# Expert down product with the activations held: four products of 128 columns a chunk, sum with tokens in partitions

## The reference, cut to what matters

```
probs = softmax(x @ gate_w.T)                     # 32 experts
comb  = the 8 largest of probs, over their sum    # 0 elsewhere
for each expert e (width 64):
    g, u = split(x @ gate_up_w[e].T, 2)
    out += (u * silu(g)) @ down_w[e].T * comb[:, e]
```

## Time and profile before

| | |
|---|---|
| median of 3 runs | 1034.54 us (1033.78 to 1035.93) |
| the profiled execution | 1029.92 us, span of the instructions 1028.2 us |
| mean granted clock of TensorE in it | 0.982 |
| TensorE, weight loads | 918.5 us busy, 631.6 us (they overlap) |
| VectorE, ScalarE, POOL | 645.9, 613.9, 658.5 us busy |
| down product (L1438) | 512 MATMULs, 263.5 us busy |
| the turn of its sum (L1359) | 64 MATMULs, 9.7 us busy |
| its copy (L1000) | 16 times, 9.5 us busy |

### The profile page before, as it was taken

One profiled execution on the slowest core, in us unless ns is written; L12 is line 12 of the kernel. 1 busy time (PEld: TensorE's weight loads), 2 busy tenths in 40 slices (PEclk: granted clock), 3 DMA queues, 4 the chain that ended last, 5 costly groups with the idle time before them and its releaser, 6 DMA issues.

```text
span 1028.2 us, 16655 instructions
## 1 busy us (share of the span) xinstructions
PE 918.5 (89%) x5472; PEld 631.6 (61%) x5472; DVE 645.9 (63%) x1444; ACT 613.9 (60%) x1869; POOL 658.5 (64%) x607
## 2 busy tenths in 40 slices
PE   3237898998999999999999999999999998999998
PEld 1024565676666566677666565678666576667665
DVE  5884785668757856778748745778744247447432
ACT  3236475687394566698475556699355459377432
POOL 5763768556668856856759855857655546645654
PEclk9998999889999999999999999999999999999999
DMA  5004343102543525530353524550153652261352
GB/s 179 1 0 96 82 85 83 42 25 53 134 104 82 117 62 123 124 83 18 76 112 83 125 55 93 119 115 18 42 126 83 125 124 55 51 144 26 83 126 61
DMA packets 63224, 85.67 MB, mean 83 GB/s; under 512 B 3681, under 2 KB 29090, under 8 KB 62882
## 3 DMA queue, kind: packets, MB, share of 16 engines
q1 hardware_dynamic: 63138, 84.61, 36.6%
HBM read 79.32 MB, written 5.28 MB: 82 GB/s over the span
## 4 chain that ended last, share of the span: by engine, by line
PE 61%; ACT 15%; DVE 6%; POOL 6%; issue 5%; DVEq 0%; ACTq 0%; POOLq 0%
PE bank L1438 17%; PE bank L1412 9%; PE bank L1414 8%; PE bank L1413 8%; ACT probs L1008 6%; PE bank L1474 3%; PE bank L1459 3%; PE bank L1488 2%; POOL work L826 2%; PE bank L1310 1%; PE bank L1316 1%; PE bank L1452 1%; ACT work L984 1%; DVE probsT L1256 1%; POOL probs L834 1%
## 5 line engine op out<-in xcount | busy, mean ns | idle before, releaser
L826 POOL TENSOR_TENSOR work<-work,spread_w 128x512 f32<-128x512 f32 x256 | 336.5, 1327 | 184.5 <-DVE work L1215 168.7
L1215 DVE TENSOR_TENSOR work<-work,bank 128x512 f32<-128x512 f32 x256 | 174.3, 682 | 234.4 <-ACT work L984 151.7
L1438 PE MATMUL bank<-work,down_w 128*128 128x512 f32 x512 | 263.5, 598 | 9.0 <-ACT yT L1000 5.6
L984 ACT ACTIVATE work<-bank 128x512 f32<-128x512 f32 x256 | 151.0, 596 | 183.1 <-PE bank L1414 180.3
L1008 ACT ACTIVATE probs<-bank,neg_max 128x96 f32<-128x96 f32 x512 | 166.0, 385 | 10.6 <-DVE neg_max L1242 9.0
L1412 PE MATMUL bank<-z_hi,gate_hi 128*128 128x512 f32 x256 | 168.9, 660 | 0.0
L834 POOL TENSOR_TENSOR probs<-probs,prob_inv 128x768 f32<-128x768 f32 x64 | 94.1, 1471 | 74.7 <-DVE prob_inv L1250 74.7
L1008 ACT ACTIVATION_READ_ACCUMULATOR probs<-bank,neg_max 128x1 f32 x512 | 127.3, 251 | 0.0
L1438 PEld LDWEIGHTS bank<-work,down_w 128*128 128x128 f32 x512 | 95.3, 190 | 38.1 <-POOL work L826 9.8
L1414 PE MATMUL bank<-z_hi,gate_lo 128*128 128x512 f32 x256 | 102.7, 401 | 0.0
L1412 PE MATMUL bank<-z_hi,up_hi 128*128 128x512 f32 x256 | 102.1, 399 | 0.0
(11 more groups left out here) (142 smaller groups left out, 1484.3 us busy)
## 6 DMA issues: line engine op xcount, KB each, us to landing
spread_w<-comb_dram SPq DMA_DIRECT2D x128, 512.0 KB, 6.7
vals<-v_dram SPq DMA_DIRECT2D x16, 384.0 KB, 4.1
x_buf<-x SPq DMA_DIRECT2D x8, 256.0 KB, 3.4
v_dram<-v_tok SPq DMA_DIRECT2D x8, 256.0 KB, 4.7
out<-xs SPq DMA_DIRECT2D x8, 256.0 KB, 3.8
spread_w<-wg SPq DMA_DIRECT2D x1, 1024.0 KB, 7.2
spread_w<-wu SPq DMA_DIRECT2D x1, 1024.0 KB, 9.2
comb_dram<-combT SPq DMA_DIRECT2D x16, 64.0 KB, 1.6
```

What stands on the lines that cost most here:

```text
L826: pool.tensor_tensor(work[:, n % WORK], work[:, n % WORK], spread_w[:, n // EACH % 2, s % EACH], ALU.mult).then_inc(hid_gated, 1)
L984: act.activation(work[:, n % WORK], bank[GATE_BANKS[ring_of(row, f, s)]], ACT.Silu).then_inc(silu_ready, 1)
L1215: dve.tensor_tensor(work[:, n % WORK], work[:, n % WORK], bank[UP_BANKS[ring_of(row, f, s)]], ALU.mult).then_inc(gated_ready, 1)
L1438: pe.matmul(bank[Y_BANK], down_w[:, c], work[:, n % WORK], start=(c == 0), stop=(c == CH - 1)).then_inc(down_done, 1)
```

## The change

The down product holds 128 tokens of `work` and streams `down_w[:, c]`, four times a chunk. The sum has tokens in partitions, as x has. The copy and the turn go, with `yT`, `y_copied` and the y_back steps of all tables. VectorE adds bank 6 to x directly (y_add), and this add now frees bank 6: the first down product of a stage and the first mix of an attention part wait for `moe_done`. y_add stands where y_copy stood in time, but on VectorE: at slot 3 before gated, in an attention part behind the maxima of the second tile.

```diff
@@ scalar
-            def y_copy(fg):
-                act.wait_ge(down_done, (fg + 1) * CH)
-                act.activation(yT[:], bank[Y_BANK], ACT.Copy).then_inc(y_copied, 1)
...
-                        if s == LAG and not starts_stream(row, f):
-                            y_copy(STAGE_AT[row, f] - 1)
...
-                        if i == f[0]:
-                            y_copy(end - 1)
...
-            y_copy(len(STREAM) - 1)
@@ vector
-            def y_back(row, f):
-                x = x_of(row) if f < G else xs
-                add_side(x, x, f % G, row, "y_back", f, moe_done, STAGE_AT[row, f] + 1)
+            def y_add(fg):
+                row, f = STREAM[fg]
+                dve.wait_ge(down_done, (fg + 1) * CH)
+                x = (x_of(row) if f < G else xs)[:, T * (f % G):T * (f % G) + T].rearrange("p t d -> p (t d)")
+                dve.tensor_tensor(x, x, bank[Y_BANK], ALU.add).then_inc(moe_done, 1)
...
+                        if s == LAG and not starts_stream(row, f):
+                            y_add(STAGE_AT[row, f] - 1)
...
+                        if i == f[0]:
+                            y_add(END_AT[row, i] - 1)
...
-            y_back(ROWS - 1, MOE - 1)
+            y_add(len(STREAM) - 1)
@@ tensor
-            def y_back(row, f):
-                pe.wait_ge(y_copied, STAGE_AT[row, f] + 1)
-                side_free(row, "y_back", f)
-                for t in range(T):
-                    mm = pe.transpose(side[:, P * t:P * (t + 1)], yT[:, P * t:P * (t + 1)], ident[:])
-                mm.then_inc(side_ready, 1)
...
-                    wait(pe, y_copied, n // CH)
+                    wait(pe, moe_done, n // CH)
...
-                pe.matmul(bank[Y_BANK], down_w[:, c], work[:, n % WORK], start=(c == 0),
-                          stop=(c == CH - 1)).then_inc(down_done, 1)
+                for t in range(T):
+                    cols = slice(P * t, P * (t + 1))
+                    mm = pe.matmul(bank[Y_BANK][:, cols], work[:, n % WORK, cols], down_w[:, c], start=(c == 0 and t == 0),
+                                   stop=(c == CH - 1 and t == T - 1), skip_group_check=True)
+                mm.then_inc(down_done, 1)
...
-                    pe.wait_ge(y_copied, END_AT[row, i])
+                    pe.wait_ge(moe_done, END_AT[row, i])
```

More of the change, by code:

```diff
@@ L64 @@
 Y_BANK, SIDE_BANK = 6, 7
-IN_SIDE = ("x_turn", "qkv", "attnT", "mlp1", "mlp2", "moe_turn", "route", "weighT", "y_back",
+IN_SIDE = ("x_turn", "qkv", "attnT", "mlp1", "mlp2", "moe_turn", "route", "weighT",
            "seq_turn", "keys", "queries", "values", "proj")
@@ L112 @@
         8: own(("route", 1), ("r_sum", 1)) + ahead(("wred", 1)),
-        9: own(("top", 1), ("y_back", 0)),
+        9: own(("top", 1)),
         10: own(("weigh", 1)) + ahead(("kvsum", 2)),
@@ L126 @@
         4: back(("m_apply", 3)) + ahead(("h_newton2", 0), ("h_rg", 0)),
-        5: back(("y_back", 2)) + ahead(("h_scale", 0)),
+        5: ahead(("h_scale", 0)),
         6: back(("moe_turn", 3), ("z_hi", 3)) + ahead(("h_sq2", 0)),
@@ L144 @@
         4: ahead(("m_apply", 0)),
-        5: own(("y_back", 1)) + ahead(("kvsum", 5)),
+        5: ahead(("kvsum", 5)),
         6: ahead(("moe_turn", 0), ("z_hi", 0)) + own(("s_stats", 1), ("s_rstd", 1)),
@@ L157 @@
     "attn": {
-        8: back(("y_back", 3)),
         26: own(("proj", 0)),
@@ L161 @@
     "attn_lo": {
-        5: own(("y_back", 1)),
         6: own(("s_stats", 1), ("s_rstd", 1)),
@@ L165 @@
     "attn_hi": {
-        5: back(("y_back", 3)),
     },
@@ L194 @@
         3: ahead(("h_scale", 0), ("qscale", 1), ("attend", 4)),
-        4: own(("y_back", 0)) + ahead(("h_sq2", 0)),
+        4: ahead(("h_sq2", 0)),
         5: own(("s_stats", 0), ("s_rstd", 0)) + ahead(("h_red2", 0), ("h_pow2", 0)),
@@ L210 @@
         2: own(("s_rstd", 1)),
-        3: own(("y_back", 1), ("s_stats", 1)),
+        3: own(("s_stats", 1)),
         4: own(("s_apply", 1)) + ahead(("attend", 6)),
@@ L254 @@
         9: own(("route", 1), ("r_sum", 1)) + ahead(("wred", 1)),
-        10: own(("top", 1), ("y_back", 0)),
+        10: own(("top", 1)),
         11: own(("weigh", 1)) + ahead(("kvsum", 2)),
@@ L267 @@
         4: ahead(("h_newton1", 0)),
-        5: back(("y_back", 2), ("m_apply", 3)) + ahead(("x_turn", 1), ("h_newton2", 0), ("h_rg", 0)),
+        5: back(("m_apply", 3)) + ahead(("x_turn", 1), ("h_newton2", 0), ("h_rg", 0)),
         6: own(("values", 0)) + ahead(("h_scale", 0)),
@@ L288 @@
         4: back(("m_apply", 3)),
-        5: back(("y_back", 2)) + own(("queries", 0)),
+        5: own(("queries", 0)),
         6: back(("moe_turn", 3), ("z_hi", 3)),
@@ L325 @@
     (ROWS, "fourth"): {
-        5: back(("y_back", 2)),
     },
@@ L407, in every_step @@
             yield from slot_steps(period, place, at)
-    yield ROWS - 1, "y_back", MOE - 1
 ORDER = list(every_step())
@@ L483, in hybrid_block @@
         work = sb("work", [P, WORK, GT])
-        yT = sb("yT", [P, GT])
         seqT, keysT = sb("seqT", [P, WIN + SEQ]), sb("keysT", [P, WIN + SEQ])
@@ L528, in hybrid_block @@
         silu_ready, gated_ready, hid_gated = sem("silu_ready"), sem("gated_ready"), sem("hid_gated")
-        down_done, y_copied, moe_done = sem("down_done"), sem("y_copied"), sem("moe_done")
+        down_done, moe_done = sem("down_done"), sem("moe_done")
         scores_ready, max_ready, probs_ready = sem("scores_ready"), sem("max_ready"), sem("probs_ready")
@@ L1220, in _ @@
                      "h_red1": h_red1, "h_newton1": h_newton1, "h_newton2": h_newton2, "h_scale": h_scale, "h_red2": h_red2, "h_sum": h_sum, "mlp2": mlp2,
-                     "z_lo": z_lo_step, "r_sum": r_sum, "top": top_step, "comb": comb_step, "y_back": y_back, "proj": proj, "lead": lambda row, n: gated(row, 0, n)}
+                     "z_lo": z_lo_step, "r_sum": r_sum, "top": top_step, "comb": comb_step, "proj": proj, "lead": lambda row, n: gated(row, 0, n)}
             norm_stats(0, "x", 0)
@@ L1418, in _ @@
                      "seq_turn": lambda row, n: turn(row, "s", n, "seq_turn"), "qkv": qkv_step, "attnT": attnT_step,
-                     "mlp1": mlp1, "mlp2": mlp2, "route": route, "weighT": weighT, "y_back": y_back, "keys": keys,
+                     "mlp1": mlp1, "mlp2": mlp2, "route": route, "weighT": weighT, "keys": keys,
                      "queries": queries, "values": values, "proj": proj,
```

## The result

The changed kernel takes 1058.99 us in the median (1044.99 to 1080.40, four runs), the one before 1034.16 in the same series. The ratio is 1.0225, 95% interval 1.0158 to 1.0293: 2.2% slower, where 0.8% had been forecast, and outside the range. The profiled execution of the changed kernel is its slowest, 1080.40 us; a second profile, of 1058.11 us, stands among the experiments (after again) and is nearer to the median. The ratios in this document leave out runs more than 1.5% above the fastest of their kernel (here the one of 1080.40), so they differ a little from the quotients of the medians.

What follows compares the result with a forecast made beforehand. TensorE was taken to bound the expert stages, TensorE and ScalarE by turns the attention parts. 12 - 4.4 - 1.5 - 6.4 + 7 + 3 - 1.35 = +8.4, say +8 us: 1042.5 us, range 1032 to 1051.

Steps and rivals of the forecast that it cites:

- term 2: Transposes of the sum leave TensorE: -4.4 us in expert slots, -1.5 in attention parts; late reciprocal against freed ScalarE: 0.
- rival C: First attention part's half clock lasts longer or shows elsewhere: +6 us, 1048 us, chance 0.14; gone: 6 less, chance 0.04.
- Term 1: Down product in expert stages: four products for one cost 0.05 us a chunk over 256 chunks, loads hidden, +12 us.
- Rival D: Down product's weight loads do not hide: six more per chunk paid in full, +292 us, 1327 us, chance 0.01.
- Term 3: Side-bank waits behind the old add at 358, 592 and 817 us shrink, with less half clock: together -6.4 us.
- Term 4: y_add on VectorE delays first down products at stage boundaries: +7 us, plus +3 for half clock at the two largest.
- Rival A: VectorE's adds are not late at stage boundaries and the waits for the copy go: 1027 us, chance 0.12.
- rival B: The add's delay vanishes in later waits of the stage, with part of the four products' cost: 1036 us, chance 0.14.
- Term 5: Tail: the last add starts where the copy did, -1.35 us.

Runs made afterwards that it cites:

- after again: The changed kernel, unedited, run again on another chip: 1063.41 us, ratio 1.0324 to the kernel before; its profiled execution took 1058.11 us.
- kernel 6: The changed kernel, with six unread products on TensorE filling the idle time before each attention part's turn of probabilities: 1027.35 us, ratio 0.9963 to the kernel before.
- kernel 1: The changed kernel, with y_add moved behind the first tile's second reciprocal in attention parts: 1024.96 us, ratio 0.9935 to the kernel before.
- kernel 7: kernel 1 with ScalarE's copy to yT back at its old places and VectorE adding from yT: 1022.57 us, ratio 0.9912 to the kernel before.
- kernel 3: The kernel before, with the down product split into four products of 128 columns, weights still held, copy and turn kept: 1034.29 us, ratio 1.0024.
- kernel 2: The kernel before, with a wait and an unread 0.69 us reduction on VectorE ahead of the second reciprocal in attention parts: 1039.47 us, ratio 1.0062.
- kernel 8: kernel 1 with ScalarE's copy, and the add from yT, at four stage boundaries only: 1018.35 us, ratio 0.9896 to the kernel before.
- Kernels 4: kernel 1 with y_add earlier, at the end of slot 2, at four stage boundaries: 1019.33 us, ratio 0.9877 to the kernel before.

## Why the prediction was wrong

The direction, which had 0.75, held, but for the wrong reason: the forecast had +11 us in the expert stages and -1.5 in the attention parts, and the traces show +3 and +49 in the first profile, +5 and +26 in the second. That the sign came out right is luck: with the stages at +3 and the other terms as they stood, the sum is 3.2 - 1.5 - 1.35 = +0.3, no change.

**The step that failed** stands in term 2: the late reciprocal was named, with both its times (441.61, and 442.9 against the measured 442.74), and then "I set the two against each other: 0, bounds -1 and +1 for each of five parts". As plain delays that was nearly right: late reciprocal +1.1 (kernel 6 beside 1), ScalarE's free time -1.3 (kernel 7 beside 1). What was left out is that the delay falls on TensorE as idle time, just ahead of a stretch of small products, and that a half clock may follow it, at which TensorE is the bound of that stretch. This I had reckoned with at two stage boundaries, at 1.5 us each, and as rival C in the first attention part, at 6. The price at the parts is 0.43 us for each us of half clock, and it stayed for 10 to 48 us: that made 3.7 to 21.5 us a part (the change's parts less those of kernel 6). The forecast's profile had shown the length to be expected: 13.6 us in the first part, not 3.4.

**Term 1** (four products) was too high. 0.05 a chunk was taken from a values slot; measured are 0.035 where nothing waits, and over all stages 3.6 us for the 12 forecast (kernel 3), or 5.1 beside kernel 2. So of 256 x 0.035 = 9 us some four to five vanish in waits, where one had been forecast. That the loads hide held: 2048 MATMULs at a mean of 277 ns (forecast near 275), and 2048 loads of 192 ns. The Trainium skill's rule of the row groups (TensorE: Matmul & The Clock Gate, Part 3, The mechanism) is not borne out by this trace: eight loads of 192 ns alone are 1.54 us, and eight loads with their eight products of the same, full rows take 0.89 from their start to that of what follows (358.76 to 359.65 in the change). The Trainium skill, in the same section, also lets a load that goes into the background weight buffer run ahead of products in flight; no run here shows that buffer. Rival D, 1327 us, is refuted.

**Term 2**, the turn: the last two stages, which hold one turn, are 0.66 longer in the change and 1.10 in kernel 3, which keeps the turn. That leaves 0.44 for it, as forecast. In the attention parts kernel 7, which has the copy and not the turn, is 0.4, 0.4 and 0.9 us shorter than before in the three parts at full clock, for 0.3 forecast.

**Term 3** (waits gone): held for the waits; for the clock it was in part chance. The waits and their half clock are gone, and the group of stages that had the one at 817 is 2.8 us shorter (121.1 for 123.9). But kernels 2 and 3 still have the two longer waits (2.18 and 2.01 us, 2.04 and 1.93), and only the last of these four was followed by half clock. So the 1.3 us counted twice for the clock are a price that this one execution of the kernel before paid, not one that it always pays.

**Term 4** (late add): held. The distances across the boundaries grew by 2.40 and 2.37 in the fourth stages, for +2.5 each, by 1.57 in the third stage of period 2, for +1.5, and by 1.69 in the first row's third stage, of which 0.4 is left at the end of the two first stages (at most 0.5 forecast); the half clock behind the two largest came, for 3.4 us (6.8 behind the second one in the second profile), and a third, of 3.4, in the first row's third stage, which was not forecast. In kernel 8, where these four boundaries are released by the copy, the stages are 8.5 us shorter than in kernel 1: that is the price of the late adds with their half clock, for the 10 forecast. (The single delays of the forecast add up to 7.5, where it says 7.) The first down product waited 3.65 us as forecast (3.5 to 4), the other 3.27. Kernels 4 and 8 win part or all of it back. **Rival A** had this as its hinge, and its hinge did not hold. Of **rival B**, the delay of the adds did not vanish, but of the four products' cost about half did.

**Term 5**, the tail: -1.31 for -1.35.

With the stages' sum right (+3) and the attention's two plain delays right, the forecast would have been close to kernel 6. The clock in four attention parts is more than all of the error: 54 and 29 us in the two profiles, of which the 8 us too many in the stages hid a part. In the terms of the cases given, it was C's mechanism, at another place and at five to nine times its price, and it had 0.14. The prediction also held that 0.2% can be told from no change; the intervals of these runs reach 0.35 to 0.7% to either side.

What stays open: why the half clock lasts longer in the change (10 to 48 us) than with the same 1.3 us of idle time in the old kernel (7 to 10, kernel 2), and whether it does so as a rule. For kernel 2 this rests on one profile, with 53 us of half clock in all; its two slowest runs had some 95 us each (an estimate from their spans and mean clocks), for 114 and 158 in the two profiles of the change. Kernel 2 differs from the change in the form of the product and in ScalarE's copy, and no experiment changed one of these alone.

## What to carry to other kernels

When an operation moves to another engine's queue, read what stands behind it there and follow that to TensorE, also where the move looks like an even trade; here one place in VectorE's order was worth 3 to 4% of the kernel's time (0.9935 for 1.0225 or 1.0324). A short idle time of TensorE is to be priced with the clock that may follow it: look at what kind of stretch stands behind it, and at how long the profile's own half clocks last in stretches of that kind. If such a wait can't be removed, filling it with products that nobody reads can pay, as kernel 6 shows. And one profile is one execution: the half clocks of one and the same kernel came and went from run to run, so a term that gives back a half clock is worth its share of the runs, not the whole.

## What the runs showed of the hardware

- An idle time of 1.3 us on TensorE, ahead of a stretch of 96- and 128-column products, was followed by a granted clock of 0.50, 0.2 to 1.8 us after its end, in 11 of the 12 places that had it in three profiles (the change twice, kernel 2). With six products of 512 columns in that place the clock stayed at 1.00 in all four. Shorter ones of 0.67 and 0.74 us in the same parts were followed by half clock in 1 of 12 places (the kernel before, kernels 3 and 7).
- Idle times of 1.2 to 1.7 us among the products of the expert stages, from 300 us on, were followed by no half clock in any of 21 places in the ten profiles. Those of 3.27 to 3.66 us at the fourth stages (the change twice, kernels 1 and 6) came with it in 8 of 8, for 3.4 us in seven and 6.8 in one; it began between 1.2 us ahead of their end and 0.9 us behind it.
- At 0.50 the clock stayed for up to 47.8 us while TensorE was busy 47.80 of 47.80 us.
- Six more weight loads of 192 ns a chunk, all rows and columns used, with the same 512 columns streamed, cost 0.035 us a chunk (kernel 3, last two stages).
